# Cross attentions with natural-order float32 queries and keys: four row tiles of 32 partitions side by side, row maxima subtracted by a selector matmul

## The reference

```python
q = (x @ Wq).reshape(B, N, H, d).transpose(0, 2, 1, 3)
k = kv[:, :, 0].transpose(0, 2, 1, 3)
attn = jnp.einsum('bhnd,bhmd->bhnm', q, k) * scale
attn = softmax1(jnp.where(mask[:, None, :, :], neg, attn))
out = jnp.einsum('bhnm,bhmd->bhnd', attn, v)
out = out.transpose(0, 2, 1, 3).reshape(B, N, C)
return out @ Wproj + bproj
```

## Time and profile before

| | |
|---|---|
| median of 3 runs | 1310.36 us (1308.19 to 1311.71) |
| the profiled execution | 1310.29 us, of which its span is 1308.5 us |
| mean granted clock of TensorE | 0.873 of full speed |
| PE busy | 1080.7 us, 83% of the span |
| DVE busy | 780.1 us, 60% |
| ACT busy | 491.0 us, 38% |

### The profile page before, as it was taken

How to read it: one execution, slowest core, us unless ns; L and a number is a source line. 1 busy time by engine, 2 the same in 40 slices (tenths; PEclk the granted TensorE clock), 3 DMA queues, 4 the chain that set the end, 5 groups by cost and what they waited for, 6 DMA issues and landing times.

```text
span 1308.5 us, 14411 instructions
## 1 busy us (share of the span) xinstructions
PE 1080.7 (83%) x5072; PEld 638.1 (49%) x5072; DVE 780.1 (60%) x1999; ACT 491.0 (38%) x900; POOL 140.3 (11%) x135
## 2 busy tenths in 40 slices
PE   5778789999998886397499898789789789798983
PEld 2444366666564443265276444344444444444753
DVE  7765555565576655333745756687857767663532
ACT  4333333333224332011323444356546436454331
POOL 1000000000000111202521001010100120000222
PEclk8777779999999776699788999899889879989887
DMA  9000014000004000112100000000000000001122
GB/s 303 9 9 6 3 46 130 1 1 1 1 1 133 5 11 10 34 40 64 21 2 5 11 5 5 1 3 3 2 2 3 2 17 3 3 2 32 41 61 71
DMA packets 33232, 35.92 MB, mean 27 GB/s; under 512 B 5030, under 2 KB 23614, under 8 KB 33161
## 3 DMA queue, kind: packets, MB, share of 16 engines
q1 hardware_dynamic: 31112, 31.21, 7.9%
q0 software_dynamic: 2048, 3.79, 1.0%
HBM read 23.04 MB, written 9.70 MB: 25 GB/s over the span
## 4 chain that ended last, share of the span: by engine, by line
PE 63%; DVE 23%; issue 5%; ACT 4%; POOL 2%; DMA 2%; SPq 1%; POOLq 0%; ACTq 0%; DVEq 0%
PE PS L160 57%; DVE MX L1838 5%; DVE MX L1520 2%; PE PS L477 2%; DVE KB L1420 1%; PE PS L585 1%; SPq L2129 1%; ACT PT L1164 1%; POOL OT L2043 1%; DVE OT L1559 1%; DVE Q L1459 1%; DVE Ht L1369 1%; PE PS L983 1%; DVE st L1356 1%; DVE STG L1411 1%
## 5 line engine op out<-in xcount | busy, mean ns | idle before, releaser
L1272 ACT ACTIVATE PT<-PS 128x512 f32<-128x512 f32 x256 | 141.5, 597 | 108.7 <-PE PS L160 106.5
L160 PE MATMUL PS<-QB,KB 112*128 112x512 f32 (+1 forms) x384 | 168.6, 489 | 10.5 <-DMA QB<-MT 3.5
L160 PE MATMUL PS<-KB,QB 96*128 96x512 f32 (+1 forms) x384 | 152.8, 473 | 25.0 <-DVE MX L1838 21.8
L1838 DVE TENSOR_REDUCE MX<-PS 128x2 fp32r<-128x1024 f32 x128 | 151.8, 1217 | 13.1 <-PE PS L160 12.0
L1164 ACT ACTIVATE PT<-PS 77x512 f32<-77x512 f32 x192 | 106.8, 598 | 125.1 <-PE PS L160 123.7
L160 PE MATMUL PS<-HT,RA 128*128 128x512 f32 x288 | 130.7, 593 | 0.0
L160 PE MATMUL PS<-HT,S 128*96 128x512 f32 (+1 forms) x200 | 116.5, 686 | 12.6 <-ACT HT L1032 10.8
L160 PEld LDWEIGHTS PS<-KB,QB 96*128 96x128 f32 x384 | 72.3, 207 | 105.8 <-DVE MX L1838 45.3
L2026 POOL TENSOR_TENSOR ve<-ve,nh 128x4 f32<-128x4 f32 x40 | 41.7, 1043 | 654.2 <-DVE ve L1364 654.0
L160 PEld LDWEIGHTS PS<-RA,PT 128*128 128x128 f32 x816 | 99.0, 193 | 14.9 <-issue 14.2
L160 PEld LDWEIGHTS PS<-QB,KB 112*128 112x128 f32 (+1 forms) x384 | 69.8, 187 | 69.4 <-ACT PT L1272 36.5
(11 more groups left out here) (224 smaller groups left out, 1546.7 us busy)
## 6 DMA issues: line engine op xcount, KB each, us to landing
RA<-in_l_w SPq DMA_DIRECT2D x1, 2304.0 KB, 10.4
RB<-in_l_w SPq DMA_DIRECT2D x1, 2048.0 KB, 10.2
RA<-in_l_w SPq DMA_DIRECT2D x1, 2048.0 KB, 8.8
d<-OT SPq DMA_DIRECT2D x2, 960.0 KB, 9.1
QB<-MT SPq DMA_DIRECT2D x48, 32.0 KB, 1.9
RB<-d SPq DMA_DIRECT2D x6, 256.0 KB, 2.9
o<-PT SPq DMA_DIRECT2D x6, 256.0 KB, 2.3
dbuf<-OT SPq DMA_DIRECT2D x2, 640.0 KB, 6.2
```

Of the source, the lines that this page charges most:

```text
L160: return e.matmul(o, l, r, start=first, stop=last, skip_group_check=True)
L1272: e.activation(slot[p], PS[:, banks.of(expd, "s", s, c, j), :], ACT.Exp, bias=0.0, scale=a4.scale).then_inc(*expd("s", s, c, j))
L1838: e.tensor_reduce(Mv[par][:, t, RM + 4 * g + 2 * p2:RM + 4 * g + 2 * p2 + 2], PS[:, 2 * p2:2 * p2 + 2, :], AX, ALU.max).then_inc(*rmax("s" ...
```

## The change

Queries and keys of the three cross attentions become plain float32 in their natural order: 16 heads of 8 give 128 partitions, four heads in each block of 32 (two heads of 16 in `l0x`, which takes two such columns of 128). One projection (two in `l0x`) replaces the groups. The keys `km` stand four times, for r = 0 to 3, each masked by `a.rows[r]` so that in every block of 32 partitions one head is left. A matmul then reads 32 partitions alone, and the four blocks j = 0 to 3 are addressed as four row tiles of the array, each with its own PSUM bank. Raw scores take two row tiles at a time, into banks 0 and 1, which `hook("raw")` takes out of the rotation while cross attentions run. One reduction then reads both banks. The maxima, transposed, are copied once by DVE into MTc, and a second matmul of each row tile, with a constant selector SEL that holds -1 in row r of each block, subtracts them in PSUM. The DMA transfers of the maxima are gone for the cross attentions. The weights of `wv`, `wo` are permuted on the host to the new order of heads.

```diff
 def cross_front(i):                                            # tensor
-                for g in range(0, a.ng, 2):
-                    yield from by_turns(*(queries(a, (i,), i % 2, g + j, hT.at(i)) for j in range(2)))
+                for c in range(a.nq):
+                    k, free = banks.take(qact, i, c)
...
+                    mm(e, PS[:, k, :], a.wq[:, c, :], HTv[i % 2]).then_inc(*projected(i, c))
...
                 for t in range(4):
-                    for g0 in range(0, a.ng, a.per):
...
+                    for half in range(2):
...
+                        for c in range(a.nq):
+                            for j in range(2):
+                                p = 32 * (2 * half + j)
+                                if c == 0:
+                                    w.wait_ge(*banks.take_at(j, rmax, i, t, half))
+                                m = mm(e, PS[:, j, 308 // a.nq * c:308 // a.nq * (c + 1)], Q[p:p + 32, c, 128 * t:128 * t + 128],
+                                       a.km[p:p + 32, b, rn * c:rn * c + rn, :], True, not a.mask)
 def cross_back(i):                                             # tensor
-                w.wait_ge(*mq[i % 2].at(i))
+                w.wait_ge(*mtc.at(i))
...
+                def scores(r):
+                    k4 = []
+                    for j in range(4):
+                        k, free = banks.take(expd, i, r, j)
                         w.wait_ge(*free)
+                        k4.append(k)
+                        mm(e, PS[0:NK, k, :], a.km[32 * j:32 * j + 32, b, r, :], Q[32 * j:32 * j + 32, r * a.nq // 4, :], True, False)
+                    for j in range(4):
+                        m = mm(e, PS[0:NK, k4[j], :], SEL[32 * j:32 * j + 32, r, 0:NK], MTc[i % 2][32 * j:32 * j + 32, :], False, not a.mask)
+                        if not a.mask:
+                            m.then_inc(*scored(i, r, j))
 def cross_front(i):                                            # vector
-                        e.tensor_reduce(M[:, t, RM + g0 * a.hpg:RM + g0 * a.hpg + n], src, AX, ALU.max).then_inc(*rmax(i, t, g0))
+                        e.tensor_reduce(o, PS[:, 0:2, 0:308].rearrange("p i (r k) -> p i r k", k=NK), AX, ALU.max).then_inc(*rmax(i, t, half))
...
+                e.tensor_copy(MTc[i % 2], PS[:, banks.of(mtc, i), :]).then_inc(*mtc(i))
 def maxima(key, groups, par, queries_of):                      # sync
-                for g in groups:
-                    e.dma_start(queries_of(g)[RM:RK, :].bitcast(F32), MT[RM:RK, :].bitcast(F32)).then_inc(*mq[par](*key))
 def order(...):
-            FRONT = {"l0x": 40, "l0f": 27, "l1x": 32, "l2x": 3, "l2f": 6, "l3x": 32}
-            BACK = {"l0x": 34, "l0f": 27, "l1x": 34, "l2x": 3, "l2f": 5, "l3x": 34}
+            FRONT = {"l0x": 14, "l0f": 27, "l1x": 13, "l2x": 3, "l2f": 6, "l3x": 13}
+            BACK = {"l0x": 9, "l0f": 27, "l1x": 9, "l2x": 3, "l2f": 5, "l3x": 9}
```

More of the change, by code:

```diff
@@ L284, in program @@
[L284 to L289, removed]
+        a0 = Att(16, 1.0 / float(np.sqrt(np.float32(128))), two(wv0), two(wv0), wvp, two(S0[:, 1024:1280]),
+                 cols[:, 0:1], cols[:, 0:1], bv0, 0, "l0", expo=True)
@@ L525, in cross_front @@
                         yield
-                yield from maxima((i,), i % 2, rmax.at(i, "all"))
+                yield from maxima((i,), MXc[i % 2], rmax.at(i, "all"))
             def back(i):
@@ L1014, in hook @@
             def hook(name):
-                if name == "self":
+                if name == "raw":
+                    banks.order = [k for k in banks.order if k > 1]
+                elif name == "no raw":
+                    banks.order += [0, 1]
+                elif name == "self":
                     banks.order = [4, 5, 6]
@@ L1065, in keys @@
-                m.then_inc(*kcA(n))
-                yield
-            def prepare(a):
-                for g0 in range(0, a.ng, 2):
-                    yield from by_turns(*(keys(a, a.n0 + g, g, CK, lambda hh, g=g: kall[:, g * a.hpg + hh, :]) for g in (g0, g0 + 1)))
+                        e.activation(EK[c], P, ACT.Identity, bias=a.bk, scale=1.0).then_inc(*kact(a.n0, c))
+                    w.wait_ge(*kact.at(a.n0, c))
+                    w.wait_ge(*ld["c"].all())
+                    if a.n0 == 2:
+                        w.wait_ge(*scored.at(3, 3, 3))
@@ L1071, in prepare @@
+                    for r in range(1, 4 // a.nq, 2):
+                        r += c * 4 // a.nq
+                        m = e.activation(a.km[:, :, r, :], EK[c][:, :, 0:NK], ACT.Copy, scale=a.rows[r])
+                    m.then_inc(*kcA(a.n0, c))
+                yield
                 for b in range(NB):
@@ L1507, in cross_front @@
                 a = att[kind]
-                for g in range(0, a.ng, 2):
-                    yield from by_turns(*(queries(a, (i,), g + j, queries_at(i, g + j)) for j in range(2)))
-                M = Mv[i % 2]
+                yield from idle(a.nq)
+                M = MXc[i % 2]
                 w.wait_ge(*mx_free((i,)))
@@ L2228, in hook @@
                     w.wait_ge(*vproj.at("l0", 3))
-                    load("l3x", w3, A["l3x_w"])
+                    load("l3x", w3[:, 0:512], A["l3x_w"])
                 elif name == "l1x0":
```

532 lines of the change are left out of this document (269 added, 263 removed).

## The result

| | before | after |
|---|---|---|
| median | 1311.03 us (1308.19 to 1316.84, 4 runs) | 1347.80 us (1346.80 to 1352.21, 4 runs) |
| ratio of after to before | | 1.0281, 95% interval 1.0239 to 1.0323 |
| span of the profiled execution | 1308.5 us | 1345.3 us |
| mean granted clock of TensorE | 0.873 | 0.851 |

The change made the kernel 2.8% slower, where the prediction had it 3.2% faster: 1347.8 us, outside the range of 1230 to 1305. `units[i]` is numbered through: 0 to 3 are `l0x`, 4 to 7 `l0f`, 8 to 11 `l1x`, 12 to 15 `l2x`, 16 to 19 `l2f`, 20 to 23 `l3x`. Unit 8 is woven into the end of `l0f`, unit 20 into the end of `l2f`.

A forecast was written before the change was run, and what follows sets the result against it. Waits between PE's pieces (key splits on DVE and ACT, transfers of the maxima) were taken to bound it. `l0x` -42.7, `l1x` 0, `l3x` +1.7, elsewhere -1.6 and +1: -41.6 on 1310.3, 1268 us, range 1230 to 1305.

The forecast's parts named there:

- preparation: Start of `l0x`: loses sixteen splitting steps and most masked copies, gains selector and memset; -8 us (bounds -4 and -10).
- two full units: `l0x` units with front, back and tail: 33 us each (30 to 36) against 43.7, -10.7 twice.
- drain: The 24.0 us behind the full `l0x` units lose most of the wait for transfers: -6 us.
- unit 9: First full `l1x` unit without a tail: table load and exponentials ahead of its queries, 26 us against 20.7, +5.3.
- the row tiles side by side: Scores on PE: four row tiles run together, about 1.2 us a group with selector; tiles in turn had chance 0.07.
- the ladder: Raw scores through banks 0 and 1, PE alternating with DVE's reduction: eight steps of 1.70 us, 13.6; with masks 15.7.
- ACT's order ahead of the first raw group: Full `l0x` unit: four exponentials precede the two of the queries, so raw scores start 7.7 us after the turned rows.
- at the better clock of their stretches 31 against 31.9 and 29.5 against 26.8 (estimates): `l3x` units with a tail: 2 to 3 us longer than the one without, but at a better clock.
- the 28 us of the unit without a tail: `l3x`: 7.7 + 15.7 + 2.1 + 2.5 = 28 us against 23.9, with masks in scores and ladder.
- PSUM and the clock give nothing back: Rival: clock falls in `l1x` and `l3x`, scores wait for banks, every unit 2 us longer; 1292 us, chance 0.17.
- "+1" for banks: Units sharing banks with raw scores, as inside `l0f` and `l2f`, have two banks fewer: +1 us.
- the cheaper ladder: Rival: handover 0.12 us, not 0.34, saves 21 us in twelve units, another 8 at full clock; 1238 us, chance 0.2.

The follow-up runs named there:

- ACT's order: Changed kernel, in six `l1x` and `l3x` units the previous unit's first four exponentials moved behind the copy of the queries: 1315.03 us, ratio 0.9998.
- The stretches by themselves: Changed kernel plus six kinds of matmul run without waits behind the last output, each after a pause; one execution, two row tiles 24.9 us, one tile 41.2.
- the pair in the kernel before: Kernel before, two constant float32 matmuls added ahead of each raw group of `l3x`: 1335.52 us with 128 rows, 1421.97 us with 32.
- the two other pairs: Same reorder of exponentials, added to reductions one step earlier (1337.72 to 1307.32 us), and to that plus four raw banks (1332.54 us without earlier reductions; all three 1302.49).
- An order one step earlier: Changed kernel, reductions of raw scores one step earlier among DVE's silu products in units 8 and 20: 1337.72 us, ratio 1.0162.
- the change in `l0x` alone, with its first ladder widened: Kernel before with the change only in `l0x`, exponentials behind query copies in units 1 to 3, four raw banks in unit 0: 1271.20 us, ratio 0.9646.

## Why the prediction was wrong

| | forecast, us | profiled, us |
|---|---|---|
| `l0x`: preparation, units 0 and 1 | -8, 0, -7.3 | -3.1, -3.0, -2.4 |
| `l0x`: two full units, drain | -21.4, -6 | -27.4, -3.2 |
| unit 8 (in `l0f`) | none | +13.9 |
| unit 9; units 10 and 11 | +5.3; -5.3 | +5.5; -2.1 |
| from the last `l1x` maxima to the rows of unit 12 | none | +4.8 |
| unit 20 (in `l2f`) | none | +13.4 |
| units 21 to 23, end of `l3x` | +1.7 | +42.4 |
| everything else | -0.6 | -2.1 |
| sum | -41.6 | +36.8 |

- **Right**: the row tiles side by side (1.25 us a scores group, forecast 1.2), the ladder (1.70 us a step at full clock, forecast 1.70), the reduction (798 ns, forecast 0.79 us), the chain in `l0x` without transfers, and ACT's order ahead of the first raw group. That `l0x` as a whole came to -39.1 us, forecast -42.7, is in part luck: preparation and unit 1 gave 9.8 us less than forecast, and the two full units 6.0 more, with 29.2 and 30.8 us where I took 33 for a clock of 0.77; it was 1.00 and 0.94, and why it rose was not tested.
- **The step that failed** is "at the better clock of their stretches 31 against 31.9 and 29.5 against 26.8 (estimates)", with the 28 us of the unit without a tail, which holds 2.5 us for the clock. The units took 38.3, 35.3 and 44.7 us. I carried the clock of the earlier trace rows over to another instruction mix. With the change the clock of `l3x` is 0.61 to 0.83, and at 1.2 GHz a ladder step with masks costs 2.92 us and not 1.96. ACT's order, worth 33 us in the kernel, shows that the pause ahead of the first raw group, which the forecast priced as a wait alone, lets the clock fall in unit 21 (0.61 with it, 0.87 without). The stretches by themselves show that work on one or two row tiles can leave TensorE at 1.2 GHz with PE busy, and the pair in the kernel before that work on 32 rows can pull the clock down without a pause. That the low clock of `l3x` after the pause comes from the raw groups' few rows is argued from these, not shown in the kernel itself: in `l0x` the clock came back with raw groups of the same form. How the 42.4 us split between pause, rows and ladder is not settled: ACT's order alone gave back 17 of them in units 21 to 23 (10 and 11 in the two other pairs), and what was left went with a clock still at 0.79 to 0.87.
- The rival "PSUM and the clock give nothing back" named the clock for `l1x` and `l3x`, but priced it at 2 us a unit; in unit 21 it was ten times that.
- **The second step** is the cost of raw groups inside `l0f` and `l2f`, taken as nothing but "+1" for banks. The prediction said that everything behind a waiting raw group queues on PE, and did not apply it where DVE is full: four waits of PE, 6.2 us in all, for reductions behind the silu products. An order one step earlier takes 11.7 of unit 8's 13.9 us away (8.3 against the 66.0 us that this unit took with ACT's order).
- Unit 1 gained less than forecast, with its clock at 0.60; why the preparation did was not looked into. Unit 9 came out as forecast, from the same reasoning on ACT's order that I did not follow into the clock, but its sum holds nothing for the clock, which went from 1.00 to 0.87 there, so the agreement is in part luck.
- Two sums of the prediction are off by a little: its terms for `l3x` add up to +1.9 and not +1.7, and the cheaper ladder to 1239 us and not 1238. Nothing hangs on it.

## What to carry to other kernels

Price new matmuls at the clock that they themselves will get, not at that of the stretch they go into: in unbroken work a row tile alone, or two at a time, ran at half clock here with PE busy throughout. Work out the sum at half clock as well, as a rival. All four tiles at once reached full clock in unbroken work, but are no cure by themselves: raw scores on four tiles left unit 20 at 0.73 and the first `l0x` unit at 0.53. Where one engine's copy releases PE, put it ahead of that engine's batch work for the unit before; here that order alone was worth the whole loss. And where a change pays in one stage and costs in two, keep it in the one: the change in `l0x` alone, with its first ladder widened, is 3.5% faster than the kernel before.

## What was unexpected of the hardware

- Float32 matmuls on one row tile of 32 rows kept TensorE at 1.2 GHz for 41.2 us of unbroken work, two tiles at a time for 24.9 us; four tiles at a time, 112 rows in float32r and 128 rows in float32 reached 2.4 GHz in the same execution.
- Added to units that ran at 0.91 to 1.00, two float32 matmuls of 32 by 128 columns ahead of each raw group pulled the clock of the whole unit down to 0.64 and 0.65, and the units to about twice their length: 51.4 and 58.8 us against 23.9 and 31.9, where the same columns on 128 rows gave 30.1 and 38.5.
- Four float32 row tiles side by side cost 0.85 us a group in unbroken work, as much as one full float32 matmul of 512 columns there (18.7 us / 22 = 0.85). One row tile alone took 41.2 us / 24 = 1.72 us at half clock, which would be 0.86 at full (an estimate): four times, in float32.
The Trainium skill ("TensorE: Matmul & The Clock Gate", Part 3, measured speedup) gives 3.07 times for four; the measurement here decides for this form.
- Between other work of a unit a raw group of two tiles took 0.72 us at full clock; in a stretch of its own, 24.9 us / 24 = 1.04 at half clock, which would be 0.52 at full (an estimate, as it never ran there). Where the difference comes from was not tested.
